# One masking instruction over three diagonal blocks instead of three, on GpSimd

## The chip, the cores and the metric

The kernel runs on one core of one Trainium2 chip. The metric is the device time of one launch in microseconds. Before the change the median of 3 runs is 2373.58 us (2372.36 to 2376.29).

## What is computed

The input is 8 sequences of 512 tokens with 256 features. Four layers of masked linear attention ("retention"), each with a gated projection, a group normalisation, a GELU network and a layer normalisation, are followed by a mixture of 8 experts. The part that matters here is the causal mask:

```python
k, q, v = jnp.split(x @ wkqv, 3, axis=-1)
qkt = jnp.einsum('bid,bjd->bij', q, k) / jnp.sqrt(jnp.float32(d))
row_norm = 1.0 + jnp.sqrt(jnp.arange(s, dtype=x.dtype))[None, :, None]
r = jnp.tril(qkt) / row_norm
denom = jnp.clip(jnp.abs(r.sum(-1, keepdims=True)), 1.0, None)
r = r / denom
return jnp.einsum('bij,bjd->bid', r, v)
```

## The kernel before

TensorE, VectorE (DVE), ScalarE (ACT), GpSimd (POOL) and the DMA queue of SyncE each run a program of their own. The order of work on each engine is written out by hand in the `body` of that engine; semaphores tie the engines together. The sequences go in two slots, A and B. A step handles one sequence in each slot; there are 4 layers with 4 steps, so 16 steps of some 61 us, up to about 1040 us of the span. In a step slot A works through the attention of its sequence while slot B finishes the second half of its earlier one, and then the roles change. After the steps comes the expert part, which holds none of the code that is changed.

Every fp32 product is made of three matmuls (`mm3`, lines 1954 to 1958) on operands split in a high and a low half: `hi*hi`, `hi*lo`, `lo*hi`. So each intermediate result is copied to its high half by ACT, and its low half is the difference, made by DVE or POOL.

The scores of a sequence are computed transposed, in four blocks of 128 rows (key positions). Block `b` holds columns `b*128` to 511 only (`LO`), and only the first 128 columns of these, its diagonal block, need the mask. For each block in turn TensorE computes it (`scores`), ACT copies the high half (`high_p`, line 1030), DVE subtracts for the low half (`low_p`, line 1342 to 1344, reported as line 1314 of its helper) and adds 1 to `p_lo`, and POOL masks the diagonal block in both halves (`mask_scores`, line 814 to 823, two `affine_select` of 128 columns each) and adds 1 to `p_masked`.

TensorE multiplies the masked scores with the input in `retain` (lines 2027 to 2037). Its weights, which are loaded ahead of each matmul, are the 128x128 pieces of the scores:

```python
for b in range(TB):
    for k in range(b, TB):
        if k == b:
            pe.wait_ge(p_masked[s], at.base + b + 1)
        elif b == 0:
            pe.wait_ge(p_lo[s], at.base + k + 1)
        ins = mm3(score_bank(s, k)[:, 0:D + 2], both(pf_sp[s], ALL, b, cols(k)), both(h_sp[s], ALL, b), b == 0, b == k)
```

Of its 30 matmuls 12 belong to block 0; the 13th is the first that needs block 1 masked. In slot A `retain` comes right behind the scores. In slot B `up_projection` of slot A (24 matmuls of 512 columns) stands between them.

Behind `retain` of slot A TensorE goes on with `up_projection` of slot B (lines 2089 to 2107, matmuls on line 2100 first). It waits for `y_hi` of slot B, which ends a chain on DVE (`groupnorm_out`, lines 1413 to 1448: instructions on lines 1429, 1431, 1419, 1424) and ACT (`high_y`, line 1055).

On POOL the order in slot A is: mask block 0, `rstd_group` of slot B (line 827), mask blocks 1 to 3, then a wait for `y_lo` of slot B. In slot B it is: mask blocks 0 to 3, then `split_f` of slot A (line 798).

Of the kernel before, what the change touches and what calls it, by code (L numbers as in the profile page):

```python
# [23 lines left out]
ALU = mybir.AluOpType  # L24
# [3 lines left out]
P = 128  # L28
# [6 lines left out]
def f32(ap):  # L35

    return ap.bitcast(F32)


def hold(eng, held):  # L40

    eng.sem_inc(held, 1)
# [9 lines left out]
def network(nc, x, xT, WkqvT, Wm1, Wm2, Wf1, Wf2, layer_cols, ln_g, ln_b,  # L52
# [7 lines left out]
    B, S, D = x.shape  # L60
    L = WkqvT.shape[0]
    DC = D // P
    TB = S // P
# [3 lines left out]
    A_, B_ = 0, 1  # L67
# [5 lines left out]
    LO = [0, P, 2 * P, 3 * P]  # L73
# [36 lines left out]
    with ExitStack() as ctx:  # L110
# [3 lines left out]
        def sem(name):  # L114
            return ctx.enter_context(nc.semaphore(name))

        def sems(name):
            return [sem(f"{name}{s}") for s in range(SLOTS)]
# [49 lines left out]
        base = nc.sbuf_base  # L168
# [18 lines left out]
        def halves(name, s, shape, at):  # L187
            size = (4 * shape[1] * shape[2] + 127) // 128 * 128
            return [place(f"{name}{n}{s}", shape, at + n * size, F32R) for n in range(2)]
# [6 lines left out]
        pf_sp = [halves("pf_sp", s, [P, FC, S], WORK[s] + 36 * KB + 256) for s in range(SLOTS)]  # L196
# [68 lines left out]
        held = sem("held")  # L265
# [9 lines left out]
        def split_count(name, layer):  # L275
            return layer * len(SPANS) + list(SPANS).index(name) + 1
# [18 lines left out]
        s_psum, p_hi, p_lo, p_masked = sems("s_psum"), sems("p_hi"), sems("p_lo"), sems("p_masked")  # L295
# [147 lines left out]
        def layernorm_gain(eng, ops, s, at, at_z, pieces=WHOLE):  # L443

            gain = lnv[s][:, 0:D].unsqueeze(1).to_broadcast([P, TB, D])
            eng.wait_ge(lnv_loaded[s], at.layer * (2 * DMA) + 2 * DMA)
            eng.wait_ge(z_normed[s], at.base + U)
            for k in pieces:
                ins = ops.tensor_tensor(out=at_z[:, k, :], in0=at_z[:, k, :], in1=gain[:, k, :], op=ALU.mult)
            ins.then_inc(z_gained[s], U)  # L450

        def layernorm_bias(eng, ops, s, at, at_z, pieces=WHOLE):

            bias = lnv[s][:, D:2 * D].unsqueeze(1).to_broadcast([P, TB, D])
            eng.wait_ge(z_gained[s], at.base + U)
            eng.wait_ge(h_stored[s], at.it * DMA + DMA)
            for k in pieces:
                ins = ops.tensor_tensor(out=h_out[s][:, k, :], in0=at_z[:, k, :], in1=bias[:, k, :], op=ALU.add)
            ins.then_inc(h_new[s], U)

        def layernorm_out(eng, ops, s, at):

            layernorm_gain(eng, ops, s, at, z[s][:, :, :], BLOCKS)
            layernorm_bias(eng, ops, s, at, z[s][:, :, :], BLOCKS)
# [318 lines left out]
        def _(pool):  # L783
            for s in range(SLOTS):
# [4 lines left out]
                                    base=0, pattern=[[-1, P]], channel_multiplier=1).then_inc(pool_consts, 1)  # L789
# [10 lines left out]
            def split_weight(name, l):  # L800
                pool.wait_ge(w_hi, high_count(name, l))
                at = SPANS[name]
                for a in range(0, at.stop - at.start, D):
                    part = slice(a, a + D)
                    ins = nc.gpsimd.tensor_tensor(out=wide(1, name)[:, part], in0=raw[:, at.start + a:at.start + a + D],
                                                  in1=f32(wide(0, name)[:, part]), op=ALU.subtract)
                ins.then_inc(w_lo, 1)

            def split_h(s, at):
                pool.wait_ge(h_hi[s], at.base + U)  # L810
                for k in range(TB):
                    low_half(h_sp[s][1][:, k, 0:D], h_in[s][:, k, :], h_sp[s][0][:, k, 0:D], h_lo[s], 1)

            def mask_scores(s, at, blocks):
                for b in blocks:
                    pool.wait_ge(p_lo[s], at.base + b + 1)
                    hold(pool, held)
                    for half in range(2):
                        part = pf_sp[s][half][:, b, LO[b]:(b + 1) * P]
                        ins = nc.gpsimd.affine_select(  # L820
                            out=part, in_=f32(part), compare_op=ALU.is_ge, fill=0.0, base=LO[b] - b * P,
                            pattern=[[1, (b + 1) * P - LO[b]]], channel_multiplier=-1)
                    ins.then_inc(p_masked[s], 1)

            def rstd_group(s, at):
                pool.wait_ge(g_var[s], at.base + U)
                nc.gpsimd.tensor_tensor(out=gsm[s][:, 5:6], in0=gsm[s][:, 5:6], in1=neg_half[:, 0:1], op=ALU.pow).then_inc(g_rstd[s], U)

            def layernorm_rstd(s, at):

                pool.wait_ge(z_var[s], at.base + U)
                nc.gpsimd.tensor_tensor(out=zr[s][:, 0, :], in0=zr[s][:, 0, :], in1=neg_half[:, :], op=ALU.pow).then_inc(z_rstd[s], 2)
                pool.wait_ge(z_rstd[s], at.base + 2)
                nc.gpsimd.tensor_tensor(out=zr[s][:, 1, :], in0=zr[s][:, 0, :], in1=zr[s][:, 1, :], op=ALU.mult).then_inc(z_rstd[s], 2)

            def split_f(s, at):
                for c in range(FC):
                    pool.wait_ge(f_hi[s], at.base + c + 1)
                    low_half(pf_sp[s][1][:, c, :], tmp[s][:, c, :], pf_sp[s][0][:, c, :], f_lo[s], 1)
# [19 lines left out]
            def inverse_root(n):  # L859
                pool.wait_ge(var_ready, n + 1)  # L860
                nc.gpsimd.tensor_tensor(out=rstd[n % 2][:, :], in0=rstd[n % 2][:, :], in1=neg_half[:, :], op=ALU.pow).then_inc(rstd_ready, 1)  # L861
# [25 lines left out]
            def body(now, before, earlier, seam, last=False, turn=True):  # L887
                if seam:
                    split_weight("qk", now.layer)
                if earlier:  # L890
                    layernorm_rstd(B_, earlier)
                split_h(A_, now)
                if seam:
                    split_weight("vm", now.layer)
                mask_scores(A_, now, (0,))
                if before:
                    rstd_group(B_, before)
                mask_scores(A_, now, (1, 2, 3))
                if before:
                    pool.wait_ge(y_lo[B_], before.base + U)  # L900
                    if seam:
                        split_weight("m2", now.layer)
                    if earlier:
                        layernorm_gain(pool, nc.gpsimd, B_, earlier, z[B_][:, :, :], BLOCKS)
                    split_f(B_, before)
                    layernorm_rstd(A_, before)
                    if earlier:
                        layernorm_bias(pool, nc.gpsimd, B_, earlier, z[B_][:, :, :], BLOCKS)
                    split_h(B_, now)
                    if last:  # L910
                        inverse_root(0)
                else:
                    pool.wait_ge(w_lo, split_count("vm", 0))
                    for name in ("m2", "f1", "f2"):
                        split_weight(name, 0)
                    split_h(B_, now)
                if seam:
                    split_weight("f1", now.layer)
                rstd_group(A_, now)
                if seam:  # L920
                    split_weight("f2", now.layer)
                if last:
                    sum_weights(0)
                mask_scores(B_, now, range(TB))
                if last:
                    inverse_root(1)
                split_f(A_, now)
                if last:
                    sum_weights(1)
                if before:  # L930
                    layernorm_out(pool, nc.gpsimd, A_, before)

            run_steps(pool, body)
            for m in range(3):
                low_token(0, m)
# [7 lines left out]
            for w in range(QUADS):  # L943
                p, i = w // QPP, w % QPP
# [1436 lines left out]
```

## Time and profile before

| | us |
|---|---|
| median of 3 runs | 2373.58 |
| lowest, highest | 2372.36, 2376.29 |
| the profiled execution, its own time | 2376.31 |
| its span, first to last instruction | 2374.6 |
| TensorE busy in the span | 2347.3 |

The page of the profile gives busy times, groups of instructions and the chain that ended last. The timeline lists instructions with start and duration; `xN` means N instructions of one form merged, and brackets give the idle time of the engine before and what ended it. PE is a matmul, PEld a weight load. A matmul starts a little behind its weight load, and the next one starts before the recorded end of the one before.

### The profile page before, as it was taken

The numbers are of one execution on the slowest core, as the hardware profiler recorded it, in microseconds if no ns is written. First come the engines' busy times: TensorE is split into PE (matmuls) and PEld (weight loads), VectorE is DVE, ScalarE is ACT, GpSimd is POOL, SyncE is SP. The second block draws the span as 40 slices with busy tenths as digits, with TensorE's granted clock in tenths as the row PEclk, the third lists the DMA queues.
The fourth block names the chain that finished last, engine by engine and source line by source line (L and its number), as shares of the span: only waits on it lengthen the run. The fifth ranks groups of instructions, "written<-read, shape, count | busy, mean of one in ns | idle before, by whom it ended". The sixth has DMA issues, their size and how long they took to land. (4 is left out here: it accounts for less than half of the span.)

```text
span 2374.6 us, 34431 instructions
## 1 busy us (share of the span) xinstructions
PE 2347.3 (99%) x11146; PEld 1957.5 (82%) x11146; DVE 1637.5 (69%) x2971; ACT 1333.7 (56%) x2319; POOL 1429.3 (60%) x1565
## 2 busy tenths in 40 slices
PE   9999999999999999999999999999999999999998
PEld 7888888888888888878888888888888888888886
DVE  3677777777777777878887756665656756574545
ACT  5666766676666766656555544444444444444443
POOL 2366765566556756668888855556555556455544
PEclk9999999999999999999999999999999999999999
DMA  7234454445444443246667656464465454454342
GB/s 252 55 98 106 103 138 107 102 107 138 112 106 107 112 110 107 66 151 218 239 202 234 215 195 197 160 191 156 162 190 188 164 172 159 163 195 168 142 155 76
DMA packets 410545, 357.24 MB, mean 150 GB/s; under 512 B 284944, under 2 KB 373264, under 8 KB 394000
## 3 DMA queue, kind: packets, MB, share of 16 engines
q1 hardware_dynamic: 409408, 354.44, 48.5%
q8 instruction: 82, 1.34, 0.2%
q10 hardware_dynamic: 976, 0.81, 0.1%
q14 instruction: 79, 0.65, 0.1%
HBM read 250.99 MB, written 104.20 MB: 150 GB/s over the span
## 5 line engine op out<-in xcount | busy, mean ns | idle before, releaser
L872 POOL TENSOR_TENSOR hid_lo<-full,hid_hi 128x512 fp32r<-128x512 f32 x384 | 505.7, 1330 | 500.2 <-ACT full L1145 457.2
L1658 DVE SCALAR_TENSOR_TENSOR full<-ps,bias_cols,sum 128x512 f32<-128x512 f32 x384 | 288.1, 750 | 200.5 <-PE ps L1958 182.9
L1956 PE MATMUL ps<-hid_hi,m_w 128*128 128x512 f32 x1024 | 399.6, 390 | 0.1
L1958 PE MATMUL ps<-hid_hi,m_w 128*128 128x512 f32 x1024 | 398.5, 389 | 0.0
L1957 PE MATMUL ps<-hid_lo,m_w 128*128 128x512 f32 x1024 | 398.4, 389 | 0.0
L1142 ACT ACTIVATE hid_hi<-ps,bias_cols 128x512 fp32r<-128x512 f32 x128 | 88.3, 690 | 506.8 <-PE ps L1958 506.8
L1956 PE MATMUL ps<-te_hi,m_w 128*128 128x512 f32 x896 | 351.6, 392 | 2.5 <-DVE sum L1645 1.4
L1958 PE MATMUL ps<-te_hi,m_w 128*128 128x512 f32 x896 | 349.3, 390 | 0.0
L1957 PE MATMUL ps<-te_lo,m_w 128*128 128x512 f32 x896 | 349.2, 390 | 0.0
L1956 PEld LDWEIGHTS ps<-hid_hi,m_w 128*128 128x128 f32 x1024 | 192.2, 188 | 40.5 <-issue 0.5
L1958 PEld LDWEIGHTS ps<-hid_hi,m_w 128*128 128x128 f32 x1024 | 192.2, 188 | 40.2
L1957 PEld LDWEIGHTS ps<-hid_lo,m_w 128*128 128x128 f32 x1024 | 192.2, 188 | 39.8
L1149 ACT ACTIVATE hid_hi<-full 128x512 fp32r<-128x512 f32 x256 | 162.0, 633 | 93.2 <-DVE full L1658 93.2
L1956 PEld LDWEIGHTS ps<-te_hi,m_w 128*128 128x128 f32 x896 | 168.3, 188 | 43.1 <-DVE sum L1645 5.0
L1958 PEld LDWEIGHTS ps<-te_hi,m_w 128*128 128x128 f32 x896 | 168.5, 188 | 35.2
L1957 PEld LDWEIGHTS ps<-te_lo,m_w 128*128 128x128 f32 x896 | 168.4, 188 | 34.1
L798 POOL TENSOR_TENSOR pf_sp<-tmp,pf_sp 128x512 fp32r<-128x512 f32 x128 | 174.6, 1396 | 30.5 <-ACT pf_sp L1063 30.4
L820 POOL TENSOR_SCALAR_AFFINE_SELECT pf_sp<-pf_sp 128x128 fp32r<-128x128 f32 x256 | 69.0, 311 | 185.2 <-DVE pf_sp L1314 183.1
L1645 DVE TENSOR_TENSOR sum<-ps,sum 128x512 f32<-128x512 f32 x128 | 88.2, 689 | 133.7 <-PE ps L1958 125.5
L885 POOL TENSOR_TENSOR m_acc<-m_acc,out_scaled 128x512 f32<-128x512 f32 x125 | 169.5, 1356 | 1.3 <-DVE out_scaled L1675 1.3
L1649 DVE TENSOR_TENSOR sum<-ps,sum 128x512 f32<-128x512 f32 x128 | 88.1, 688 | 118.5 <-PE ps L1958 118.3
L1150 ACT ACTIVATE full<-full 128x512 f32<-128x512 f32 x256 | 159.2, 622 | 0.0
(210 smaller groups left out, 5577.5 us busy)
## 6 DMA issues: line engine op xcount, KB each, us to landing
m_w<-prepared SPq DMA_DIRECT2D x96, 1408.0 KB, 6.0
prepared<-m_w SPq DMA_DIRECT2D x32, 1408.0 KB, 5.9
h_store<-h_out SPq DMA_DIRECT2D x32, 512.0 KB, 3.2
we_raw<-in_W SPq DMA_DIRECT2D x64, 256.0 KB, 6.4
gate_bc<-gate_rows SPq DMA_DIRECT2D x64, 256.0 KB, 6.3
z<-z_store SPq DMA_DIRECT2D x30, 512.0 KB, 3.9
hT_store<-turned_h SPq DMA_DIRECT2D x96, 128.0 KB, 3.4
h_in<-h_store SPq DMA_DIRECT2D x24, 512.0 KB, 4.8
```

The costliest lines, as they stand in the source:

```text
L798: nc.gpsimd.tensor_tensor(out=lo, in0=full, in1=f32(hi), op=ALU.subtract).then_inc(done, n)
L872: nc.gpsimd.tensor_tensor(out=hid_lo[:, k, :], in0=full[:, k, :], in1=f32(hid_hi[:, k, :]), op=ALU.subtract).then_inc(hid_ready, 1)
L885: nc.gpsimd.tensor_tensor(out=at, in0=at, in1=out_scaled[:, j, :], op=ALU.add).then_inc(acc_added, 1)
L1142: nc.scalar.activation(hid_hi[:, k, :], src, ACT.Relu, bias=bias)
L1149: nc.scalar.activation(hid_hi[:, k, :], src, ACT.Relu)
L1150: nc.scalar.activation(full[:, k, :], src, ACT.Relu).then_inc(relu_ready, 1)
L1645: nc.vector.tensor_tensor(out=sum2[:, :], in0=bank_b, in1=sum1[:, :], op=ALU.add).then_inc(sums, 1)
L1649: nc.vector.tensor_tensor(out=sum3[:, :], in0=bank_b, in1=sum1[:, :], op=ALU.add).then_inc(sums, 1)
L1658: nc.vector.scalar_tensor_tensor(out=full[:, k, :], in0=src, scalar=b1_col(e, 2 * fp + BLOCK_ROW[k]), in1=other[:, :], op0=ALU.add, op1=AL ...
L1956: nc.tensor.matmul(out, w[0], x[0], start=first, stop=False, skip_group_check=True)
L1957: nc.tensor.matmul(out, w[0], x[1], start=False, stop=False, skip_group_check=True)
L1958: return nc.tensor.matmul(out, w[1], x[0], start=False, stop=last, skip_group_check=True)
```

## The change

`mask_scores` becomes two functions. `mask_first` does block 0 as before. `mask_rest` waits for the low halves of all four blocks, then masks blocks 1 to 3 in one `affine_select` per half: 3 pieces of 128 columns that lie 640 columns apart (a three-dimensional access), and adds 3 to `p_masked` at once.

```diff
-            def mask_scores(s, at, blocks):
-                for b in blocks:
-                    pool.wait_ge(p_lo[s], at.base + b + 1)
-                    hold(pool, held)
-                    for half in range(2):
-                        part = pf_sp[s][half][:, b, LO[b]:(b + 1) * P]
-                        ins = nc.gpsimd.affine_select(
-                            out=part, in_=f32(part), compare_op=ALU.is_ge, fill=0.0, base=LO[b] - b * P,
-                            pattern=[[1, (b + 1) * P - LO[b]]], channel_multiplier=-1)
-                    ins.then_inc(p_masked[s], 1)
+            def mask_first(s, at):
+                pool.wait_ge(p_lo[s], at.base + 1)
+                hold(pool, held)
+                for half in range(2):
+                    part = pf_sp[s][half][:, 0, 0:P]
+                    ins = nc.gpsimd.affine_select(out=part, in_=f32(part), compare_op=ALU.is_ge, fill=0.0, base=0,
+                                                  pattern=[[1, P]], channel_multiplier=-1)
+                ins.then_inc(p_masked[s], 1)
+
+            def mask_rest(s, at):
+
+                pool.wait_ge(p_lo[s], at.base + TB)
+                hold(pool, held)
+                for half in range(2):
+                    flat = pf_sp[s][half][:, :, :].rearrange("p b q -> p (b q)")
+                    part = flat[:, P:TB * S].rearrange("p (b w) -> p b w", w=S + P)[:, :, S:S + P]
+                    ins = nc.gpsimd.affine_select(out=part, in_=f32(part), compare_op=ALU.is_ge, fill=0.0, base=0,
+                                                  pattern=[[0, TB - 1], [1, P]], channel_multiplier=-1)
+                ins.then_inc(p_masked[s], TB - 1)
...
-                mask_scores(A_, now, (0,))
+                mask_first(A_, now)
                 if before:
                     rstd_group(B_, before)
-                mask_scores(A_, now, (1, 2, 3))
+                mask_rest(A_, now)
...
-                mask_scores(B_, now, range(TB))
+                mask_first(B_, now)
+                mask_rest(B_, now)
```

## Rows read from the trace of the kernel before

**Rows 1.** The page: busy us by engine, share of the span, instructions.

```profile
PE 2347.3 (99%) x11146; PEld 1957.5 (82%) x11146; DVE 1637.5 (69%) x2971; ACT 1333.7 (56%) x2319; POOL 1429.3 (60%) x1565
```

**Rows 2.** View of line 820: count, ns minimum/median/maximum, first and last start in us.

```profile
L820 POOL TENSOR_SCALAR_AFFINE_SELECT pf_sp<-pf_sp x256: 289/297/1279, 21.9 to 989.9; 128x128 fp32r<-128x128 f32 x128
```

**Rows 3.** Timeline of TensorE, slot A, one step: start, duration.

```profile
396.67 0.34 PE L1956 MATMUL ps<-h_sp,pf_sp 128*128 128x258 f32 x1
...
398.05 0.19 PEld L1956 LDWEIGHTS ps<-h_sp,pf_sp 128*128 128x128 f32 x1
...
400.07 0.19 PEld L1958 LDWEIGHTS ps<-h_sp,pf_sp 128*128 128x128 f32 x1
400.47 0.30 PEld L2100 LDWEIGHTS ps<-ry_sp,w_plain 128*128 128x128 f32 x2 [0.21 <-issue]
```

**Rows 4.** Timeline of POOL in the same stretch.

```profile
395.75 0.54 POOL L820 TENSOR_SCALAR_AFFINE_SELECT pf_sp<-pf_sp 128x128 fp32r<-128x128 f32 x2 [7.51 <-DVE pf_sp L1314]
396.26 0.55 POOL L827 TENSOR_TENSOR gsm<-gsm,neg_half 128x1 f32<-128x1 f32 x1
396.95 1.52 POOL L820 TENSOR_SCALAR_AFFINE_SELECT pf_sp<-pf_sp 128x128 fp32r<-128x128 f32 x6
```

**Rows 5.** Timeline of DVE and of ACT in the same stretch.

```profile
394.89 0.69 DVE L1314 TENSOR_TENSOR pf_sp<-ps,pf_sp 128x512 fp32r<-128x512 f32 x1 [0.22 <-ACT pf_sp L1030]
...
396.23 1.24 DVE L1314 TENSOR_TENSOR pf_sp<-ps,pf_sp 128x384 fp32r<-128x384 f32 x3
397.39 0.36 DVE L1429 TENSOR_SCALAR gsm<-lc,gsm 128x2 f32<-128x2 f32 x1
397.67 0.32 DVE L1431 SCALAR_TENSOR_TENSOR gsm<-gsm,lc 128x2 f32<-128x2 f32 x1
...
398.76 0.75 DVE L1424 SCALAR_TENSOR_TENSOR y<-tmp,gsm,hT_sp 128x512 f32<-128x512 f32 x1
...
399.60 0.63 ACT L1055 ACTIVATE ry_sp<-y 128x512 fp32r<-128x512 f32 x1 [1.50 <-DVE y L1424]
```

**Rows 6.** Timelines of TensorE and ACT, a step outside the inner loops.

```profile
337.24 0.63 ACT L1055 ACTIVATE ry_sp<-y 128x512 fp32r<-128x512 f32 x1 [1.49 <-DVE y L1424]
...
337.72 0.19 PEld L1958 LDWEIGHTS ps<-h_sp,pf_sp 128*128 128x128 f32 x1
337.94 0.30 PEld L2100 LDWEIGHTS ps<-ry_sp,w_plain 128*128 128x128 f32 x2
```

**Rows 7.** Timelines of DVE, POOL and TensorE, slot B, one step.

```profile
429.51 1.68 DVE L1314 TENSOR_TENSOR pf_sp<-ps,pf_sp 128x512 fp32r<-128x512 f32 x4
...
430.37 2.02 POOL L820 TENSOR_SCALAR_AFFINE_SELECT pf_sp<-pf_sp 128x128 fp32r<-128x128 f32 x8 [5.96 <-DVE pf_sp L1314]
433.07 1.59 POOL L798 TENSOR_TENSOR pf_sp<-tmp,pf_sp 128x512 fp32r<-128x512 f32 x1 [0.68 <-ACT pf_sp L1063]
...
434.91 0.28 PE L1956 MATMUL ps<-h_sp,pf_sp 128*128 128x258 f32 x1
```

**Rows 8.** Timelines of POOL and DVE where an instruction of one held up the other.

```profile
926.20 1.45 POOL L820 TENSOR_SCALAR_AFFINE_SELECT pf_sp<-pf_sp 128x128 fp32r<-128x128 f32 x2
...
926.72 0.78 DVE L1314 TENSOR_TENSOR hT_sp<-hT_in,hT_sp 128x512 fp32r<-128x512 f32 x1
...
1138.96 1.30 DVE L1663 SCALAR_TENSOR_TENSOR hid_lo<-full,hid_hi 128x512 fp32r<-128x512 f32 x1
...
1139.66 1.19 POOL L850 TENSOR_TENSOR we_raw<-we_raw 128x256 f32<-128x256 f32 x1
...
1140.18 2.16 DVE L1498 TENSOR_TENSOR m_w<-we_raw,m_w 128x1408 fp32r<-128x1408 f32 x1
...
1140.93 1.72 POOL L855 TENSOR_TENSOR we_raw<-we_raw 128x128 f32<-128x128 f32 x1
```

**Rows 9.** Timelines of POOL and TensorE where TensorE waited for POOL.

```profile
996.70 1.33 POOL L798 TENSOR_TENSOR pf_sp<-tmp,pf_sp 128x512 fp32r<-128x512 f32 x1
...
998.09 0.19 PEld L1956 LDWEIGHTS ps<-pf_sp,w_plain 128*128 128x128 f32 x1 [0.76 <-POOL pf_sp L798]
```

## The prediction

> **What bounds the kernel now.** I read the busy times first: TensorE is busy 2347.3 of 2374.6 us [rows 1]. So time is lost or won only where TensorE stands still, and an instruction saved on POOL (60% busy) is worth nothing by itself. The question is whether TensorE can be made to wait for the masks. No wait of TensorE for line 820 shows anywhere in the waits view or in the view of that line, so at present the masks are hidden in both slots; what they have is a margin, and the timelines give it.
>
> Next I read slot A's timeline. I set t = 0 at the first matmul of `retain`, 396.67 [rows 3]. The weight load of its 13th matmul, the first that needs block 1 masked, starts at 398.05, t = 1.38. POOL masks block 1 from 396.95, t = 0.28, in the first two of six selects, which follow each other every (1.52 - 0.30)/5 = 0.245 us [rows 4]. Block 1 is finished at 0.28 + 0.245 + 0.30 = 0.83, so it has 0.55 us to spare. The same times, within 0.02 us, stand in 15 of the 16 steps. The first step of the launch doesn't count: two folds of weights stand between its scores and its `retain`.
>
> In slot B `up_projection` of the other slot stands in between. The eight selects run from 430.37 to 432.39, and the 13th matmul is at 434.91 [rows 7]: 2.5 us to spare.
>
> **Part 1: the wait for all four blocks, slot A.** The low half of block 3 is finished when the last of the three subtractions ends, 396.23 + 1.24 = 397.47, t = 0.80 [rows 5]. POOL starts 0.17 us after the end of the subtraction that releases it (394.89 + 0.69 = 395.58 to 395.75) [rows 4, 5]. So the first long select starts at t = 0.98 instead of 0.28. Behind the waiting select nothing on POOL is urgent: its next work there waits for a later product of DVE and ACT until 5.6 us after the masks. `rstd_group` stands before the wait and isn't held.
>
> **Part 2: the duration d of a select of 384 columns.** No select of that size is in the trace. One of 128 columns takes 0.297 us [rows 2]. How much of that grows with the columns can be read where POOL was held up by DVE. The select that ends at 926.20 + 1.45 = 927.65 ran on for 0.15 us after DVE's operation ended at 927.50 [rows 8]. POOL's two-input operation of 256 columns ran on for 0.59 us (1140.85 against 1140.26), the one of 128 columns for 0.31 us (1142.65 against 1142.34) [rows 8]. So there 128 columns are worth 0.28 us and 0.03 to 0.04 us is a fixed tail. Take that tail off the select's 0.15 us and its 128 columns are worth 0.11 us. That gives d = 0.30 + 2 x 0.11 = 0.52 us. Ends: nothing per column, 0.30; the columns as dear as in the two-input operation, 0.30 + 2 x 0.28 = 0.86. The whole 0.15 us taken as columns gives 0.60. I take 0.52, since those 0.15 us come from this same instruction.
>
> The Trainium skill's "GPSIMD Engine Reference", section "Performance versus the Vector engine", has 1.03 cycles for an element of a body with up to two operations and about 1.8 in its best general case, at 1.2 GHz. By the first, 256 more columns are 0.22 us, as the rows have it; by the second 0.38 us, d = 0.68, and an estimate of the whole by that page would be 2385.4 us. No row of this trace shows the select at 384 columns, so the rows above decide.
>
> **Part 3: what TensorE loses.** Two selects in a row end 0.05 us closer than twice their duration (0.297 against the spacing of 0.245). The pair ends at t = 0.98 + (d - 0.05) + d, and TensorE's load starts 0.06 us after POOL's end (998.03 to 998.09) [rows 9]. Against 1.38 the delay is 2d - 0.40 us, rounded: 0.64 us with d = 0.52. All later diagonal blocks are masked by then too, so it is one wait in a step. 15 x 0.64 = 9.6 us.
>
> **Part 4: what gives some of it back.** Behind `retain` TensorE already waits a little for `y_hi` of slot B. Weight loads in `retain` are 0.12 us apart; after 400.07 the next could start at 400.19 and starts at 400.47, 0.28 us late [rows 3]. In six steps, those in the inner loops, it is so. In the other nine ACT ends at 337.87 and the load follows at 337.94, against 337.72 + 0.12 = 337.84: 0.10 us late [rows 6]. The chain to `y_hi` (group norm on DVE, then ACT) doesn't depend on `retain` of this slot. If TensorE comes later it finds it ready. That returns 6 x 0.28 + 9 x 0.10 = 2.6 us. All that comes later in a step starts from TensorE's own results and moves along with it. Net 9.6 - 2.6 = 7.0 us.
>
> **Part 5: slot B and the rest, at nothing.** Block 0 is masked as before, until about 430.37 + 0.245 + 0.30 = 430.91. The low halves end at 429.51 + 1.68 = 431.19 [rows 7], so the long pair starts at 431.36 and ends at 431.36 + 0.47 + 0.52 = 432.35, against 432.39 before. TensorE needs it at 434.9 and POOL's next work starts at 433.07, held by ACT. The cover is 2.5 us; were it gone, the pair would cost what Part 3 has. The four saved selects per step and the saved semaphore instructions lie in POOL's idle time.
>
> **A collision that decides the upper side.** DVE and POOL exclude each other for some operations. In the rows above a select of 0.297 us took about 0.74 because DVE was subtracting two SBUF tensors, and it ended only after it [rows 8]. The Trainium skill's "SBUF — State Buffer", section "SBUF: two separate sides", calls the shared port pair an exclusive lock for the whole instruction against a DVE operation with two SBUF inputs; the trace agrees. In slot A the next large such operation of DVE is line 1424 (0.75 us) at 398.76, t = 2.09 [rows 5]. It may come earlier: lines 1429 and 1431 take 0.36 and 0.32 us for two columns beside the selects, which leave that place, so up to some 0.25 us, t = 1.84. A select works on its columns from about 0.297 - 0.15 = 0.15 us after its start. With d = 0.52 the second starts at 1.45, holds the ports from 1.60 and ends at 1.97: it goes first, DVE waits at most 0.13 us, and TensorE no longer waits for DVE's chain there.
>
> **The rivals.**
> 1. *Hidden after all.* The select costs hardly more at 384 columns. With d = 0.30 the delay is 0.20 us, 15 x 0.20 = 3.0, less 2.6 given back: 2374.0 us. For it: half of the 0.297 us is certainly not columns. Against it: 0.15 us after the release are hard to explain by a tail when another operation's is 0.04. It stays within 4.7 us up to d = 0.445 (15 x 0.49 - 2.6 = 4.7).
> 2. *One instruction in name only.* The three pieces are worked off one after another with the cost of an instruction each, 0.245 us: d = 0.79, or the columns are as dear as in the two-input operation: d = 0.86. Delay 1.18 us or 1.32, so 15.1 or 17.2 us: 2388.7 to 2390.8. The second select would reach the ports at 0.98 + 0.74 + 0.15 = 1.87 or later, just behind DVE's 1.84. If it loses, it ends at 1.84 + 0.75 + 0.04 + at least 0.33 = 2.96, the delay is 1.64 us, and the time is 2373.6 + 24.6 - 2.6 = 2395.6. Against it: nothing in the trace shows a cost per piece; the trace has no such access on POOL.
> 3. *Faster.* Freed of the selects, DVE's chain to `y_hi` starts 0.25 us sooner, and the waits of Part 4 go. That gains 2.6 us: 2371.0. It decides if the pair costs TensorE nothing, so if it ends by t = 1.32; starting at 0.98 even two selects of today's 128 columns end at 1.53. Only if POOL could start long before the last low half, which the wait forbids, would this be reached. To pass 0.2% it would have to gain also elsewhere, and I see no place.
>
> **How the numbers follow.** The profiled execution took 2376.31 us, 2.7 above the median of the runs; the sum puts the changed kernel's at 2383.3, and the median at 2373.6 + 7.0 = 2380.6. The forecast's own range, d from 0.45 to 0.60, is 2378.5 (15 x 0.50 - 2.6 = 4.9) to 2383.0 (15 x 0.80 - 2.6 = 9.4). Chances: forecast 0.63, up to rival 2's lower edge and a dearer column (d 0.60 to 0.75, 2383 to 2388) 0.10, rival 1 0.14, rival 2 0.10, rival 3 0.03. A measurement of this kernel can tell 0.2%, 4.7 us, from no change. Slower by more: 0.63 less a tenth of it for its lower edge, plus 0.10 and 0.10, some 0.77; I take off 0.03 for a return in later waits that I did not find: 0.74. Same: 0.23. Faster: 0.03. The range has to leave out no more than 0.2: from 2375 (most of rival 1 lies below 2377, its lowest part is left out) to 2389 (where rival 2 starts).
>
> **What would show it.** In the trace after, the waits view has a new row of TensorE (mostly PEld, line 1956) waiting for POOL's line of the long select, 15 times, some 0.6 us each. Part 1: the long select starts 0.98 us after `retain` does. Part 2: it takes 0.52 us; if 0.30, rival 1, if 0.79 or more, rival 2. The collision: both selects of slot A of one length; a second one of 1 us or more means that DVE took the ports. Part 4: the load of line 2100 follows without a gap. Part 5: no wait for it in slot B. I would be wrong most simply by the select's length, or if a wait later in the step that I take to move along with TensorE stands still and swallows the delay.

## The result: 0.28% slower, by one wait in slot A

| | before | after |
|---|---|---|
| median of 10 runs each, us | 2376.03 | 2382.40 |
| lowest, highest | 2372.36, 2376.99 | 2378.87, 2383.37 |
| profiled execution, its own time | 2376.31 | 2382.57 |
| its span | 2374.6 | 2380.8 |

The ratio is 1.0028 (95% interval 1.0020 to 1.0037). TensorE works as long as before, and the 128 instructions that POOL is spared are of no use to the time. First part 1 of the page after, against [rows 1]; then the view of line 830, the long select, against [rows 2]; then the rows of line 830 and line 798 in the waits of TensorE's weight loads (us in total, times, longest).

```profile
PE 2347.7 (99%) x11146; PEld 1956.7 (82%) x11146; DVE 1637.2 (69%) x2971; ACT 1332.7 (56%) x2319; POOL 1410.9 (59%) x1437
...
L830 POOL TENSOR_SCALAR_AFFINE_SELECT pf_sp<-pf_sp x64: 520/520/1504, 22.2 to 994.7; 128x384 fp32r<-128x384 f32 x64
...
PEld ps L1966 <- POOL pf_sp L830: 8.5, 15, 0.6
...
PEld ps L1966 <- POOL pf_sp L798: 5.4, 15, 0.8
```

A long select takes 0.520 us, and TensorE's weight loads wait for it 15 times, once in each step but the first. No such wait was there before. (The wait for line 798, `split_f`, was there: 4.8 us, 13 times.) The timeline of the same step as in [rows 3 to 5], here TensorE, POOL, DVE and ACT of the kernel after; `retain` of slot A starts at 399.98, which is t = 0:

```profile
399.98 0.34 PE L1966 MATMUL ps<-h_sp,pf_sp 128*128 128x258 f32 x1
...
402.00 0.19 PEld L1966 LDWEIGHTS ps<-h_sp,pf_sp 128*128 128x128 f32 x1 [0.57 <-POOL pf_sp L830]
402.11 0.19 PEld L1967 LDWEIGHTS ps<-h_sp,pf_sp 128*128 128x128 f32 x1
...
404.00 0.19 PEld L1968 LDWEIGHTS ps<-h_sp,pf_sp 128*128 128x128 f32 x1
404.12 0.30 PEld L2110 LDWEIGHTS ps<-ry_sp,w_plain 128*128 128x128 f32 x2
...
400.95 0.99 POOL L830 TENSOR_SCALAR_AFFINE_SELECT pf_sp<-pf_sp 128x384 fp32r<-128x384 f32 x2 [0.83 <-DVE pf_sp L1324]
...
399.55 1.24 DVE L1324 TENSOR_TENSOR pf_sp<-ps,pf_sp 128x384 fp32r<-128x384 f32 x3
400.70 0.22 DVE L1439 TENSOR_SCALAR gsm<-lc,gsm 128x2 f32<-128x2 f32 x1
400.83 0.21 DVE L1441 SCALAR_TENSOR_TENSOR gsm<-gsm,lc 128x2 f32<-128x2 f32 x1
...
401.81 0.75 DVE L1434 SCALAR_TENSOR_TENSOR y<-tmp,gsm,hT_sp 128x512 f32<-128x512 f32 x1
...
402.65 0.63 ACT L1065 ACTIVATE ry_sp<-y 128x512 fp32r<-128x512 f32 x1 [1.25 <-DVE y L1434]
```

The pair of selects starts at t = 0.97 and ends at 1.96 (401.94); the load of the 13th matmul is at 2.02, where it was at 1.38 [rows 3]. Behind `retain` the load of line 2110 (line 2100 of before) now follows after the usual 0.12 us; the gaps of [rows 3] and [rows 6] are gone. DVE's two small operations take 0.22 and 0.21 us instead of 0.36 and 0.32 [rows 5], and line 1434 (1424 of before) starts at t = 1.83 instead of 2.09. It takes 0.75 us as before, though the second select runs until 1.96: no wait of DVE shows.

Adding up over the 16 steps, from the starts of the first and last matmul of each `retain` in both timelines: within `retain` of slot A +9.35 us (0.63 in 15 steps), from there to `retain` of slot B -3.33, within `retain` of slot B 0.00, from there to the next slot A +0.35, ahead of the first and behind the last -0.14. That is the 6.2 us between the spans.

### The profile page after: what moved, and what is told of

It is laid out like the page before. It is cut to its first block and busy times, and to the rows that moved or that the text cites. A ratio compares the mean times of both kernels' runs of the same rounds, so it can differ in the third digit from the quotient of the medians.

```text
span 2380.8 us, 34239 instructions
## 1 busy us (share of the span) xinstructions
PE 2347.7 (99%) x11146; PEld 1956.7 (82%) x11146; DVE 1637.2 (69%) x2971; ACT 1332.7 (56%) x2319; POOL 1410.9 (59%) x1437
## 5 line engine op out<-in xcount | busy, mean ns | idle before, releaser
L819 POOL TENSOR_SCALAR_AFFINE_SELECT pf_sp<-pf_sp 128x128 fp32r<-128x128 f32 x64 | 17.5, 292 | 184.2 <-DVE pf_sp L1324 184.1
```

## The experiments

In each the lines not shown are those of the kernel before or after, as named. I give the same sums over the 16 steps for each, against the first profile of before; "A to B" is from the last matmul of `retain` in slot A to the first in slot B. How far one execution can lie from another is shown by the last experiment; so what one step repeats weighs more here than a span.

**Slot A alone.** The kernel after, with slot B masked block by block.

```diff
-                mask_first(B_, now)
-                mask_rest(B_, now)
+                mask_scores(B_, now, range(TB))
```

> The change in slot A alone; slot B masks block by block as before. My theory: all of the loss is one wait of TensorE at the 13th matmul of retain in slot A, 0.63 us in 15 steps, less what returns behind it; slot B is covered. It expects the whole of the change: a span near 2380.8 us (2374.6 before, 2380.8 after), ratio 1.0026 to 1.0030, TensorE's waits for the long select 15 times, some 0.57 us each. The rival, that half of the loss comes from POOL's new rhythm in slot B (split_f waits longer), expects about 2377.7.

Measured: 2380.7 us against 2375.29 us of before in the same runs, ratio 1.0024 (1.0014 to 1.0033), span 2379.8. Waits of TensorE in its profile:

```profile
PEld ps L1976 <- POOL pf_sp L830: 8.5, 15, 0.6
...
PEld ps L1976 <- POOL pf_sp L798: 5.7, 15, 0.8
```

The wait is the same 15 times 8.5 us, `retain` of slot A has +9.38 us, A to B -3.24. So slot A holds the loss. The rival, half of it in slot B, falls. The ratio is a little under the 1.0026 to 1.0030 expected, and its interval holds both ends; the span is 1.0 us below the expected one, with 2.5 us less behind the last `retain`.

**Slot B alone.** The kernel after, with slot A masked block by block.

```diff
-                mask_first(A_, now)
+                mask_scores(A_, now, (0,))
...
-                mask_rest(A_, now)
+                mask_scores(A_, now, (1, 2, 3))
```

> The change in slot B alone; slot A masks block by block as before. My theory expects a span of 2374.6 us within 0.5, a ratio of 1.000, long selects of 0.52 us and no wait of TensorE for them. The rival that slot B carries half of the loss expects 2377.7. A second rival, that the longer selects of slot B collide with DVE's subtractions more often and delay split_f there, expects 0.3 to 1 us more in the three or four steps with a collision, so at most 2376.

Measured: 2373.05 us against 2375.29, ratio 0.9990 (0.9981 to 0.9999), span 2371.9. No wait for the long select shows, so slot B costs nothing. The second rival doesn't show either: five long selects of slot B were held up (0.81 to 1.51 us instead of 0.52), but TensorE's waits for `split_f` are 5.4 us in 14 times, as in the profiles of before (4.8 in 13, 5.5 in 15). What I had not expected is a small gain, and it lies in slot A, where this kernel does what the one before did: A to B -2.13 us. Its timeline of DVE, one step (`retain` at 396.07), shows the two small operations:

```profile
396.79 0.22 DVE L1450 TENSOR_SCALAR gsm<-lc,gsm 128x2 f32<-128x2 f32 x1
396.92 0.26 DVE L1452 SCALAR_TENSOR_TENSOR gsm<-gsm,lc 128x2 f32<-128x2 f32 x1
```

In 11 of the 15 steps the first takes 0.22 us, though six selects run beside it. Here DVE got through ahead of a select, and that select took 0.314 us instead of 0.292. The selects of 128 columns follow each other every 0.250 us in this kernel and every 0.245 in the one before, so they meet DVE's line some ns later. The start of the third of the six selects goes with the outcome. At t = 0.751 to 0.768, in all 30 steps of the two profiles of before, DVE waits; at 0.770 to 0.773 here DVE waits in four steps and goes first in four; at 0.779 to 0.783 it goes first in all seven. No run moved that start by itself, so this is a reading of the traces and not an experiment.

**The late wait alone.** The kernel before, with one wait more; the six selects stay.

```diff
+                pool.wait_ge(p_lo[A_], now.base + TB)
                 mask_scores(A_, now, (1, 2, 3))
```

> Slot A keeps its six selects of 128 columns but waits for all four low halves before them: the late wait without the long instruction. My theory: block 1 is masked at t = 0.98 + 0.245 + 0.30 = 1.53, the load follows at 1.58 against 1.38, 0.20 us in 15 steps = 3.0 us; DVE's chain to y_hi is freed of the selects as in the changed kernel and TensorE's waits behind retain go, 2.6 to 3.3 us back; the span is 2374.3 to 2375.0. The rival, that the late wait alone makes the loss and the length of the select hardly matters, expects 2380. A third possibility: selects 4 to 6 now lie where DVE runs its addition of two SBUF tensors (line 1424, t = 1.83); then selects 5 and 6 end near t = 3.1, still ahead of block 3 at 3.3.

Measured: 2373.89 us against 2375.29, ratio 0.9997 (0.9988 to 1.0006), span 2372.0. `retain` of slot A has +3.37 us (0.19 to 0.26 in a step), A to B -2.75: net 0.6. That the late wait alone makes the loss is out: it takes the length of the select with it. The third possibility happened, in all 15 steps: of the six selects the fifth (397.09 in a step whose `retain` starts at 395.07, so t = 2.02) was held up for 0.45 us and took 0.744 us (0.741 to 0.760 in the 15), and the sixth ended at t = 3.01. Timelines of POOL and DVE in that step:

```profile
397.09 0.74 POOL L820 TENSOR_SCALAR_AFFINE_SELECT pf_sp<-pf_sp 128x128 fp32r<-128x128 f32 x1
...
396.90 0.79 DVE L1425 SCALAR_TENSOR_TENSOR y<-tmp,gsm,hT_sp 128x512 f32<-128x512 f32 x1
```

Unrounded, the held select ends 0.15 us after DVE's addition does, as in [rows 8]. The span is 2.3 us below the lower end of the forecast; some 3.5 us less than in the first profile of before lie ahead of the first `retain` and behind the last.

**Block 1 alone, blocks 2 and 3 together.** The kernel before, slot A.

```diff
+            def mask_pair(s, at):
+                pool.wait_ge(p_lo[s], at.base + TB)
+                hold(pool, held)
+                for half in range(2):
+                    flat = pf_sp[s][half][:, :, :].rearrange("p b q -> p (b q)")
+                    part = flat[:, 2 * P + S:TB * S].rearrange("p (b w) -> p b w", w=S + P)[:, :, S:S + P]
+                    ins = nc.gpsimd.affine_select(out=part, in_=f32(part), compare_op=ALU.is_ge, fill=0.0, base=0,
+                                                  pattern=[[0, 2], [1, P]], channel_multiplier=-1)
+                ins.then_inc(p_masked[s], 2)
...
-                mask_scores(A_, now, (1, 2, 3))
+                mask_scores(A_, now, (1,))
+                mask_pair(A_, now)
```

> Slot A masks block 1 as soon as its low half is there, as before, and blocks 2 and 3 in one instruction per half behind the wait for all four; slot B as before. My theory: block 1 is masked at t = 0.83, no wait; the pair of 256 columns, 0.41 us each, runs from 0.98 to 1.75 and is needed at 2.45, no wait. DVE's lines 1429 and 1431 find POOL idle, so y_hi comes 0.2 us sooner and TensorE's wait of 0.10 to 0.28 us behind retain goes: a span of 2371.3 to 2372.0 us, 0.11 to 0.14% faster than before. The rival, that what returned in the changed kernel is only the slack that any later TensorE would find and DVE's chain isn't faster, expects 2374.6.

Measured: 2371.69 us against 2375.29, ratio 0.9990 (0.9981 to 0.9999), span 2368.1. Timeline of POOL and of DVE, one step, `retain` at 394.66:

```profile
394.94 0.54 POOL L820 TENSOR_SCALAR_AFFINE_SELECT pf_sp<-pf_sp 128x128 fp32r<-128x128 f32 x2
395.63 0.76 POOL L831 TENSOR_SCALAR_AFFINE_SELECT pf_sp<-pf_sp 128x256 fp32r<-128x256 f32 x2
...
395.38 0.22 DVE L1440 TENSOR_SCALAR gsm<-lc,gsm 128x2 f32<-128x2 f32 x1
395.51 0.22 DVE L1442 SCALAR_TENSOR_TENSOR gsm<-gsm,lc 128x2 f32<-128x2 f32 x1
```

No wait of TensorE for either select; A to B is -3.56 us. The span is below the forecast one by 3 us, but against the first profile of before 1.6 us less lie between slot B and the next slot A and 1.4 behind the last `retain`, where nothing was changed. The profile of before repeated below shows such differences too: 1.4 of the 1.6 us stand in one step, and in the same step that profile has 1.3 us less. The medians say 0.1%, as forecast.

**The same timing without a combined instruction.** The kernel before, slot A.

```diff
-                mask_scores(A_, now, (1, 2, 3))
+                mask_scores(A_, now, (1,))
+                pool.wait_ge(p_lo[A_], now.base + TB)
+                mask_scores(A_, now, (2, 3))
```

> Slot A masks block 1 at once, then waits for all four low halves and masks blocks 2 and 3 with four selects of 128 columns: the timing of one_then_two without a combined instruction. If its gain comes from POOL being idle while DVE runs lines 1429 and 1431 (t = 0.72 to 1.06), the gain is here too: these lines take 0.22 us each instead of 0.36 and 0.32, TensorE's load behind retain comes at t = 3.52 to 3.60 instead of 3.62 to 3.79, and slot A to slot B is some 3 us shorter in sum than before (3.6 in one_then_two), a ratio of about 0.999. The fourth of these selects (from 1.72) meets DVE's line 1424 at 1.83 and holds it for about 0.1 us, which TensorE doesn't see. If the gain needs fewer or longer instructions, the sum is 0 and the ratio 1.000.

Measured: 2371.81 us against 2373.88, ratio 0.9992 (0.9983 to 1.0001), span 2368.5. The trace settles what the ratio leaves open: A to B is -3.37 us, nearly that of the kernel with the pair, and DVE's operations are as short (`retain` at 394.56):

```profile
395.28 0.22 DVE L1431 TENSOR_SCALAR gsm<-lc,gsm 128x2 f32<-128x2 f32 x1
395.40 0.22 DVE L1433 SCALAR_TENSOR_TENSOR gsm<-gsm,lc 128x2 f32<-128x2 f32 x1
395.53 0.75 DVE L1421 SCALAR_TENSOR_TENSOR tmp<-ps,gsm,hT_sp 128x512 f32<-128x512 f32 x1
396.39 0.79 DVE L1426 SCALAR_TENSOR_TENSOR y<-tmp,gsm,hT_sp 128x512 f32<-128x512 f32 x1
```

The collision with line 1426 cost DVE 0.04 us (0.79 against 0.75), where I had expected 0.1. So what is gained comes from POOL's pause and not from fewer instructions.

**Both slots.** Block 1 alone and a pair for blocks 2 and 3 in slot A (`mask_pair` as above), the long select of the change in slot B.

```diff
-                mask_rest(A_, now)
+                mask_scores(A_, now, (1,))
+                mask_pair(A_, now)
```

> Slot A masks block 1 alone and blocks 2 and 3 in one pair, slot B has the pair of three blocks of the change. Slot A's gain (0.1% in the run before) with slot B covered: a ratio of 0.9985 to 0.9995, the span 2.6 to 3.6 us below that of before. The rival, that the two small gains seen in the runs with one slot changed each are real and add, expects 0.998.

Measured: 2371.68 us against 2375.02, ratio 0.9988 (0.9979 to 0.9997), span 2368.8. The ratio is as expected; the span is 5.8 us below that of before instead of 2.6 to 3.6, with 3.4 us of it ahead of the first `retain` and behind the last. A to B is -2.08 us: one step has +1.25, the other fifteen -3.33 together. Faster than both kernels, but no more so than with slot A alone: the two gains don't add. That both are the same free path for DVE fits the timelines (line 1429's operation takes 0.22 us in 14 of the 15 steps here too), but no run tests it further.

**A third long select, onto DVE's addition.** The kernel of the first experiment, slot A. The added select writes a tile that isn't read in this part, so no value changes.

```diff
                 hold(pool, held)
+                if extra:
+                    flat = pf_sp[s][0][:, :, :].rearrange("p b q -> p (b q)")
+                    part = flat[:, P:TB * S].rearrange("p (b w) -> p b w", w=S + P)[:, :, S:S + P]
+                    nc.gpsimd.affine_select(out=sum3[:, 0:3 * P].rearrange("p (b w) -> p b w", w=P), in_=f32(part),
+                                            compare_op=ALU.is_ge, fill=0.0, base=0,
+                                            pattern=[[0, TB - 1], [1, P]], channel_multiplier=-1)
```

> Slot A as in the changed kernel, but one more select of 3 x 128 columns, into a tile that is idle in this part, stands ahead of the two; slot B as before. It puts the last select on DVE's addition of two SBUF tensors. My theory with the exclusive ports: the first two start at t = 0.98 and 1.45, the second holds the ports until 1.93, DVE's line 1424 (ready at t = 1.83) takes them then, the third select has to wait until 2.65 and ends at 2.65 + 0.38 = 3.03; TensorE's load comes at 3.08 against 1.38, 1.70 us in 15 steps = 25.5, less 3.3 returned: 22 us more than before, a span near 2397. The rival, that they share the ports without waiting for each other, has the third end at 0.98 + 2 x 0.47 + 0.52 = 2.44, 1.11 us in 15 steps = 16.7, less 3.3: a span near 2388.

Measured: 2395.86 us against 2375.02, ratio 1.0086 (1.0070 to 1.0102), span 2394.7. Timelines of POOL and DVE, one step (`retain` at 404.18), and TensorE's waits:

```profile
405.16 0.52 POOL L830 TENSOR_SCALAR_AFFINE_SELECT sum<-pf_sp 128x384 f32<-128x384 f32 x1 [0.83 <-DVE pf_sp L1340]
...
406.10 1.04 POOL L836 TENSOR_SCALAR_AFFINE_SELECT pf_sp<-pf_sp 128x384 fp32r<-128x384 f32 x1
...
406.01 0.75 DVE L1450 SCALAR_TENSOR_TENSOR y<-tmp,gsm,hT_sp 128x512 f32<-128x512 f32 x1
...
PEld ps L1982 <- POOL pf_sp L836: 23.5, 15, 1.6
```

The last select takes 1.04 us instead of 0.52 and ends at 407.14, 0.38 us after DVE's addition does (406.76), at t = 2.96 (forecast 3.03). One select of 0.47 us more cost 24.42 - 9.38 = 15.0 us in 15 steps, 1.0 us each. Sharing without a wait would have given 0.47 each. The span is 20.1 us above that of before, against 22 forecast and 13 for the rival that shares.

**The select measured alone.** The kernel before, slot B: block 0 masked over 384 contiguous columns in the high half and all 512 in the low half.

```diff
+            def mask_wide(s, at):
+                pool.wait_ge(p_lo[s], at.base + 1)
+                hold(pool, held)
+                for half, width in ((0, 3 * P), (1, 4 * P)):
+                    part = pf_sp[s][half][:, 0, 0:width]
+                    ins = nc.gpsimd.affine_select(out=part, in_=f32(part), compare_op=ALU.is_ge, fill=0.0, base=0,
+                                                  pattern=[[1, width]], channel_multiplier=-1)
+                ins.then_inc(p_masked[s], 1)
...
-                mask_scores(B_, now, range(TB))
+                mask_wide(B_, now)
+                mask_scores(B_, now, (1, 2, 3))
```

> A measurement of the select alone: in slot B, where it is covered, block 0 is masked over 384 contiguous columns in the high half and 512 in the low half, which changes no value. If only the columns count, 384 contiguous ones take the 0.52 us that three pieces of 128 take, and 512 take 0.63 us (0.114 us for 128). If each piece costs something of its own, the contiguous 384 take less than 0.52. The time of the whole stays as before within 0.5 us.

```profile
432.31 0.51 POOL L830 TENSOR_SCALAR_AFFINE_SELECT pf_sp<-pf_sp 128x384 fp32r<-128x384 f32 x1 [5.98 <-DVE pf_sp L1324]
...
432.78 0.61 POOL L830 TENSOR_SCALAR_AFFINE_SELECT pf_sp<-pf_sp 128x512 fp32r<-128x512 f32 x1
...
PEld ps L1966 <- POOL pf_sp L798: 9.4, 20, 0.8
```

Unrounded, the two take 0.506 and 0.614 us in this step, 0.505 to 0.508 and 0.612 to 0.615 in all 16: 0.107 to 0.109 us for 128 columns, and three pieces cost 0.014 us more than 384 columns in one. A cost of an instruction for each piece, as in my second rival, doesn't exist. The expectation on the time missed: the one run gave 2379.73 us (before: 2372.17 to 2377.43). The masks of slot B end 0.5 us later, and TensorE waits 20 times for `split_f` behind them, 9.4 us in all, instead of the 15 times and 5.5 us of the repeated profile below; from slot B to the next slot A it is +3.15 us. The step of slot B shown in [rows 7] doesn't explain it, for there POOL stands idle for 0.7 us between the masks and `split_f`. Not so everywhere: in the first profile of before POOL goes on without a pause (0.05 us or less) in six of the 16 steps and after 0.3 us in three. One of the six, POOL of the kernel before and then of this one:

```profile
306.92 2.02 POOL L820 TENSOR_SCALAR_AFFINE_SELECT pf_sp<-pf_sp 128x128 fp32r<-128x128 f32 x8 [1.92 <-DVE pf_sp L1314]
308.98 1.30 POOL L798 TENSOR_TENSOR pf_sp<-tmp,pf_sp 128x512 fp32r<-128x512 f32 x1
...
309.17 1.51 POOL L820 TENSOR_SCALAR_AFFINE_SELECT pf_sp<-pf_sp 128x128 fp32r<-128x128 f32 x6
310.65 1.79 POOL L798 TENSOR_TENSOR pf_sp<-tmp,pf_sp 128x512 fp32r<-128x512 f32 x1
```

In these nine steps `split_f` starts 0.2 to 0.7 us later against `retain` than before, and they hold 3.0 of the 3.15 us. So slot B's cover against POOL's next work is thinner than that against the 13th matmul, and in six steps there is none.

**The kernel before, once more.**

> The kernel before, unchanged, profiled once more. The run with slot B alone changed showed in most steps of its unchanged slot A that DVE's line 1429 took 0.22 us instead of 0.36 and TensorE's load behind retain came at t = 3.52 to 3.58 instead of 3.62 to 3.79. If that comes from the changed slot B, this run shows 0.36 and 3.62 to 3.79 everywhere; if it is chance which of DVE and POOL gets the ports first, this run shows both kinds too.

Measured: 2375.78 us against 2375.02 of before, ratio 1.0003 (0.9992 to 1.0013), span 2370.5. Timelines of POOL and DVE, one step, `retain` at 393.39:

```profile
393.66 1.52 POOL L820 TENSOR_SCALAR_AFFINE_SELECT pf_sp<-pf_sp 128x128 fp32r<-128x128 f32 x6
...
394.11 0.35 DVE L1429 TENSOR_SCALAR gsm<-lc,gsm 128x2 f32<-128x2 f32 x1
394.38 0.32 DVE L1431 SCALAR_TENSOR_TENSOR gsm<-gsm,lc 128x2 f32<-128x2 f32 x1
```

All 15 steps are as in the first profile of before: 0.35 to 0.36 us, and the load of line 2100 at t = 3.61 to 3.82. So in two executions of this program DVE waits in all 30 steps: who gets the ports goes with the program here, and not with the execution. The span is 4.1 us below that of the first profile, 2.0 of it ahead of the first `retain` and 2.6 behind the last: between profiles of one kernel so much lies outside the steps. The step sums are steadier: A to B +0.16, with at most 0.19 in a step; B to A +0.33, though there single steps differ by up to 1.33 and cancel.

## Why the prediction was right

*What bounds the kernel*: right. TensorE's busy time is the same within 0.4 us, and all that counts is where it waits.

*Part 1, the late wait*: t = 0.98 forecast, 0.97 measured. *Part 2, the length*: d = 0.52 forecast, 0.520 measured. This was the term on which the case hung (0.30 to 0.86 from the rows), and reading it where POOL was held up by DVE [rows 8], so that the fixed part lies in the waiting, gave 0.11 us for 128 columns; the chip has 0.107 to 0.109 in one piece and 0.114 in several. The dearer rule of the Trainium skill that I set beside it ("GPSIMD Engine Reference", "Performance versus the Vector engine", 1.8 cycles an element, d = 0.68) doesn't hold for this select (measured 0.520); that of 1.03 cycles does.

*Part 3, the delay*: 0.64 us forecast for the load; the load is 0.64 later (2.02 against 1.38) and the matmuls 0.63, 9.35 us in all against 9.6.

*Part 4, what comes back*: 2.6 us forecast; 3.3 came back from slot A to slot B, and 3.1 with all else outside `retain` of slot A. The mechanism is as forecast, the gap ahead of line 2110 is gone. The size was a little too small: the six steps of the inner loops gave back 0.22 to 0.45 us (0.35 on average, against my 0.28), and of the nine others four gave back 0.15 to 0.21, against my 0.10. The other five scatter from a loss of 0.49 to a gain of 0.63, which is more than the change explains; why stays open. In the step of [rows 6] the second matmul behind the wait no longer starts 0.08 us late, and a second short wait, for `y_lo` ahead of the second half of `up_projection`, is gone too. I had left these two out.

*Part 5, slot B at nothing*: right for the change, shown by the run with slot B alone and the zero within its `retain`. My cover of 2.5 us was read in one step and measured to the wrong neighbour. The weight load of the 13th matmul comes 2.4 us after the masks in that step, but 0.85 to 2.4 us in the 16, and least in four steps in which DVE holds up a select. `split_f` comes 0.7 us after the masks in that step and right behind them in six others, and 0.5 us more of masking was enough to be felt. With the change the load comes 0.93 to 2.3 us after the masks, so the cover held. (The selects saved are four in each slot, eight in a step, 128 in all, not four in a step.)

*The collision*: DVE's line came at t = 1.83 (1.84 forecast), and the second select ended undelayed, with 0.520 us. That it held the ports against DVE, for up to 0.13 us, doesn't show: DVE's line took its 0.75 us. The third select of the experiment showed the price of the other order.

*The rivals*: hidden after all, no (d isn't 0.30); one instruction in name only, no (0.014 us for the pieces); faster, no, but half of its mechanism is real: DVE's line 1424 did start 0.25 us sooner. Where block 1 isn't kept waiting, as in the version with block 1 alone, that is left as a gain of about 0.1%.

*The sum*: 2380.6 forecast, 2382.4 measured, with a median of before of 2376.0 in the same runs instead of the 2373.6 of the three runs I started from. The step itself: 7.0 us forecast; 6.4 between the medians, 6.2 between the spans. So the forecast level was 1.8 us too low although the step was forecast too large: the median of before had risen by 2.4 us.

## What to carry to other kernels

An instruction saved on an engine that isn't the bound is worth nothing by itself, and if combining means waiting for the last input, the first consumer pays for all that is put in front of it: compare the end of the combined work with the first need, not with the last. Combine what is needed last (blocks 2 and 3), and let what is needed first go alone. To size an instruction that the trace doesn't show, find a row where it was held up just before its data: what remains after the release is the part that grows, but for a short tail (here 0.04 us of 0.15). And read a margin in every step before you call something covered: the one step of [rows 7] had more than most.

## What the hardware showed that I had not expected

- Small DVE operations on two columns pay for POOL's selects too: 0.22 us each without them, 0.36 and 0.32 beside them. On the way to a wait of TensorE that came to about 3 us of the whole kernel, as much as the masks' own wait with short selects. The Trainium skill's "SBUF — State Buffer", section "SBUF: two separate sides", describes the lock for a DVE operation with two SBUF inputs or in a two-port mode. The trace agrees for line 1431, which has two tensor inputs in SBUF (0.22 and 0.32 us); line 1429, with one tensor input and one scalar from SBUF, is delayed as well (0.22 and 0.36 us), and no run here shows in which mode it works.
- Selects of 128 columns follow each other every 0.244 to 0.245 us in the five profiles of kernels without a select over several pieces (before, before repeated, the late wait alone, the same timing without a combined instruction, the select measured alone) and mostly every 0.250 us in the six with one, in their unchanged places too. The few ns go with who gets the ports. The cause of the spacing stays open.
- A select of several pieces costs 0.014 us more than a contiguous one of the same 384 columns (0.520 against 0.506).
